# Edges sorted by groups of four nodes instead of by node, with digits spread in bf16 and degrees summed in the first convolution

## The reference

```python
def spline_conv(x, row, col, basis, idx, W, b):       # row = src, col = dst
    z = jnp.einsum('ni,kio->nko', x, W).reshape(N * K, Fout)
    msg = jnp.einsum('es,eso->eo', basis, z[col[:, None] * K + idx])
    out = jax.ops.segment_sum(msg, row, num_segments=N)
    deg = jax.ops.segment_sum(jnp.ones_like(msg[:, 0]), row, num_segments=N)
    return out / jnp.maximum(deg, 1.0)[:, None] + b

h = ones((N, 1))
h = elu(spline_conv(h, ..., stn1_w, stn1_b))          # "c1" and "h1" in the kernel
h = elu(spline_conv(h, ..., stn2_w, stn2_b))          # "c2"
t = elu(h @ stn3_w + stn3_b) @ stn4_w + stn4_b
new_pseudo = clip(pseudo + t[col] - t[row], 0, 1)
x = x + spline_conv(relu(layernorm(x)), ..., new_pseudo's basis, conv_w, conv_b)   # "c3"
x = x + attention over each node's incoming edges, then a gated update            # attention phase
```

## Time and profile before

| | us |
|---|---|
| median of 3 timed runs | 11155.94 |
| lowest and highest | 11149.67, 11158.07 |
| the profiled execution (its span from first to last instruction) | 12528.6 |
| of it, 523 to 3260: `sort_edges` | 2737 |
| of it, 60 to 523: counting | 463 |
| of it, 3450 to 3900: most of c1 | 450 |

### The profile page before, as it was taken

The page is one execution under the profiler, slowest core; times in us unless marked ns, Lnnn a source line. Parts: engine busy times, 40 slices in busy tenths (PEclk is TensorE's granted clock), DMA queues, the critical chain, the costliest instruction groups (busy, mean ns, idle before and its releaser), DMA issues. The chain is left out here.

```text
span 12528.6 us, 178083 instructions
## 1 busy us (share of the span) xinstructions
PE 6505.4 (52%) x38968; PEld 5397.9 (43%) x38968; DVE 7716.2 (62%) x17239; ACT 2933.1 (23%) x8407; POOL 7476.5 (60%) x7456
## 2 busy tenths in 40 slices
PE   3466666666475799999994444545555100000000
PEld 2355555555475677777764434434454100000000
DVE  9844444444498676666664444544576267777777
ACT  0011111111132344344432222322343000000001
POOL 5155555655200888888886888888800566666663
PEclk9966666666698999999997667766777555555555
DMA  1210000000733444444443333333322212221221
GB/s 41 65 36 2 2 2 2 2 2 2 14 41 50 93 93 94 92 94 95 92 93 49 50 51 53 54 50 52 54 42 34 35 49 50 51 50 48 51 54 40
DMA packets 1788557, 605.09 MB, mean 48 GB/s; under 512 B 1595943, under 2 KB 1729575, under 8 KB 1788260
## 3 DMA queue, kind: packets, MB, share of 16 engines
q1 hardware_dynamic: 1078132, 311.05, 12.8%
q0 software_dynamic: 255648, 274.30, 10.7%
q10 hardware_dynamic: 454736, 19.28, 3.0%
HBM read 430.75 MB, written 172.95 MB: 48 GB/s over the span
## 5 line engine op out<-in xcount | busy, mean ns | idle before, releaser
L1222 PE MATMUL c_acc<-c_spread_sb,c_basis_sb 128*125 128x256 f32 (+1 forms) x12544 | 2599.2, 376 | 1502.8 <-issue 655.0
L1222 PEld LDWEIGHTS c_acc<-c_spread_sb,c_basis_sb 128*125 128x125 f32 x12544 | 2266.5, 231 | 1803.5 <-issue 1536.3
L1614 POOL DMA_INDIRECT at_ring<-gat_table,at_place x1568 | 1585.7, 1011 | 1188.5 <-issue 1188.5
L609 POOL DMA_INDIRECT rec<-rk_rec,rk_place x1568 | 1619.3, 1033 | 1110.1 <-DVE rk_place L497 620.7
L1321 ACT ACTIVATE c_sums<-c_acc 125x512 f32<-125x512 f32 (+1 forms) x3136 | 1489.3, 490 | 2258.7 <-PE c_acc L1222 1298.6
L961 POOL DMA_INDIRECT c_ring<-hid_table,c_at x1568 | 1707.1, 1089 | 478.9 <-issue 443.2
L961 POOL DMA_INDIRECT c_ring<-feat_table,c_at x1568 | 1602.7, 1022 | 478.1 <-issue 462.9
L1084 DVE TENSOR_TENSOR c_spread_sb<-c_mark,c_rin 128x512 f32<-128x512 f32 (+1 forms) x3136 | 1745.2, 557 | 60.3
L1871 PE MATMUL gr_hps<-ident,gr_hs 128*32 128x128 f32 x98 | 29.8, 408 | 2473.7 <-issue 2066.3
L492 DVE CUSTOM_DVE_ANT_0 rk_junk_l<-rk_look_ps,rk_hi 128x98 bf16<-128x98 f32 x1568 | 402.2, 257 | 1324.1 <-remote 821.1
L1234 PE MATMUL c_mix<-c_sums,c_w 125*64 125x256 f32 (+1 forms) x9408 | 1037.3, 401 | 187.6 <-issue 133.8
(11 more groups left out here) (356 smaller groups left out, 10126.9 us busy)
## 6 DMA issues: line engine op xcount, KB each, us to landing
c_rin<-rows SPq DMA_DIRECT2D x3136, 42.0 KB
c_rin<-rows SPq DMA_DIRECT2D x3136, 20.0 KB
rows<-c_ring POOLq DMA_DIRECT2D x392, 128.0 KB
rows<-rk_blank SPq DMA_DIRECT2D x112, 252.0 KB
rows<-c_ring POOLq DMA_DIRECT2D x392, 72.0 KB
rows<-at_ring SPq DMA_DIRECT2D x196, 144.0 KB
rec<-rk_rec,rk_place POOLq DMA_INDIRECT x1568
c_ring<-hid_table,c_at POOLq DMA_INDIRECT x1568
```

The lines of the kernel that those rows point to most:

```text
L609: pool.indirect_dma_start(out=d.rec, out_offset=bass.IndirectOffsetOnAxis(ap=place[:, u, j:j + 1], axis=0), in_=rec[:, u, j, :], in_offset ...
L1222: last = pe.matmul(acc[pp % BANKS][:, (w % 2) * WN * feats:(w % 2 + 1) * WN * feats], basis[:, q, w, :, :].rearrange("p a b -> p (a b)"), ...
L1614: pool.indirect_dma_start(out=ring[:, u, j, :], out_offset=None, in_=d.gat_table, in_offset=bass.IndirectOffsetOnAxis(ap=place[:, u, j:j + ...
```

## The change

A *window* is a group of four consecutive nodes; there are 98 x 32 = 3,136 of them (`NWIN`). The change counts and sorts edges by window number (`src >> 2`) instead of by node number:

- The high digit of a window number has 25 values (`NH`) instead of 98. So `cnt_hi` and `rk_hi` are 8 x 25, the running table is [128, 25], and L396, L549, L554, L587 and L492 work on 25 columns. `c.src` in L487 is the window number.
- Rows (L530): instead of one f32 matmul of the node column with the f32 identity, two bf16 matmuls that accumulate: high digit times 128 x identity (`rk_high_ident`), and low digit times identity. ACT copies two digit columns in bf16 instead of one f32 column.
- The degree of each node no longer falls out of the count. c1's weights get a 126th column of ones (`basis_1`), `c1_w` a 126th row and a 65th column, and the 65th output of c1 is the degree; c1's output has rows of 65 values in a tensor of its own (`first_out`).
- In `count_and_prefix` the 98 block starts are taken from the loaded `starts` instead of from `c.base`, so that 12 small DVE instructions move behind the wait for that load.
- Loading has one more pass over `src` on DVE; the weight load of c1 waits for two small DVE writes.

```diff
+NWIN = NB * NW
+WBITS = WN.bit_length() - 1
+NH = -(-NWIN // P)
...
-            chain(dve.tensor_copy(c.src[:, 0:NT], c.src_i[:, :]))
...
+            chain(dve.tensor_scalar(c.key_tmp[:, :], c.src_i[:, :], WBITS, None, ALU.logical_shift_right))
+            chain(dve.tensor_copy(c.src[:, 0:NT], c.key_tmp[:, :]))
...
-        lo_hot, hi_hot = sb("cnt_lo", [P, 2, G, P], BF16), sb("cnt_hi", [P, 2, G, NB], BF16)
+        lo_hot, hi_hot = sb("cnt_lo", [P, 2, G, P], BF16), sb("cnt_hi", [P, 2, G, NH], BF16)
...
-                    dve.tensor_tensor(hi_hot[:, u, :, :], bc(c.ramp_bf[:, 0:NB].unsqueeze(1), [P, G, NB]),
-                                      bc(c.src_hi[:, at].unsqueeze(2), [P, G, NB]), ALU.is_equal).then_inc(made, 1)
+                    dve.tensor_tensor(hi_hot[:, u, :, :], bc(c.ramp_bf[:, 0:NH].unsqueeze(1), [P, G, NH]),
+                                      bc(c.src_hi[:, at].unsqueeze(2), [P, G, NH]), ALU.is_equal).then_inc(made, 1)
...
-            first = turned[0:NB, 0:P].rearrange("p (w n) -> p w n", n=WN)[:, :, 0]
-            chain(dve.tensor_copy(off[:, :], first))
+            chain(dve.tensor_copy(off[:, :], turned[0:NH, 0:P]))
...
+            dve.wait_ge(act_c, 1)
+            chain(dve.tensor_copy(block_fill[:, 0:NB], starts[:, :].rearrange("a (b w) -> a b w", w=NW)[:, :, 0]))
...
-        cols = sb("rk_cols", [P, 2, G])
+        cols = sb("rk_cols", [P, 2, 2, G], BF16)
...
-                        dve.tensor_tensor_reduce(junk_l[:, u, j, :], look[:, j % 2, 0:NB], hi_hot[:, u, j, :], 1.0, 0.0,
+                        dve.tensor_tensor_reduce(junk_l[:, u, j, :], look[:, j % 2, 0:NH], hi_hot[:, u, j, :], 1.0, 0.0,
...
-                    last = pe.matmul(rows[:, u, j, :], bc(cols[:, u, j:j + 1], [P, P]), c.ident[:, :],
-                                     start=True, stop=True)
+                    pe.matmul(rows[:, u, j, :], bc(cols[:, u, 1, j:j + 1], [P, P]), high_ident[:, :],
+                              start=True, stop=False)
+                    last = pe.matmul(rows[:, u, j, :], bc(cols[:, u, 0, j:j + 1], [P, P]), c.ident_bf[:, :],
+                                     start=False, stop=True)
...
-                            pe.matmul(look[:, j % 2, 0:NB], lo_t[:, u, j, :], table[:, k % 2, :],
+                            pe.matmul(look[:, j % 2, 0:NH], lo_t[:, u, j, :], table[:, k % 2, :],
...
-                act.activation(cols[:, u, :], c.src[:, bass.ds(g * G, G)], ACT.Copy).then_inc(cols_made, 1)
+                for k, digit in enumerate((c.src_lo, c.src_hi)):
+                    act.activation(cols[:, u, k, :], digit[:, bass.ds(g * G, G)], ACT.Copy).then_inc(cols_made, 1)
...
-                    last = pe.matmul(acc[u][:, 0:P], basis[:, u, t, :, :].rearrange("p a b -> p (a b)"), mark[:, u, t, :],
+                    last = pe.matmul(acc[u][:, 0:P], basis_1[:, u, t, :], mark[:, u, t, :],
...
-                pe.matmul(back[u][:, 0:HID], sums[:, u, :], wsb[:, :], start=False, stop=True).then_inc(mixed, 1)
+                pe.matmul(back[u][:, 0:HID + 1], sums[:, u, :], wsb[:, :], start=False, stop=True).then_inc(mixed, 1)
```

More of the change, by code:

```diff
@@ new lines, in _ @@
+            for w, slot in enumerate(SLOT_OF):
+                chain(dve.tensor_scalar(need[:, :], block_fill[:, 1:NB + 1], float(P + slot * P - 1), float(EP),
+                                        ALU.add, ALU.min))
+                chain(dve.tensor_copy(c.need[:, w, :], need[:, :]))
+                chain(dve.tensor_scalar(c.need[:, w, :], c.need[:, w, :], (slot * P).bit_length() - 1, None,
+                                        ALU.logical_shift_right))
+            chain(dve.tensor_copy(c.block_start[:, 0, :], block_fill[:, 0:NB]))
@@ L382, in _, with sums @@
             last.then_inc(counted, 1)
-            pe.matmul(count[0][:, 0:NB], c.zeros[:, 0:P], c.zeros[:, 0:NB], start=True, stop=False).then_inc(free, 2)
+            pe.matmul(count[0][:, 0:NH], c.zeros[:, 0:P], c.zeros[:, 0:NH], start=True, stop=False).then_inc(free, 2)
             pe.wait_ge(pe_ready, 1)
-            def sums(k, cnt):
-                pe.matmul(total[:, k * P:k * P + NB], c.ones[:, :], cnt, start=True, stop=True)
-                pe.matmul(within[:, k * P:k * P + NB], c.after[:, :], cnt, start=True, stop=True).then_inc(counted, 1)
-            sums(1, c.base[:, 1, :])
+            def sums(k, cnt, n):
+                pe.matmul(total[:, k * P:k * P + n], c.ones[:, :], cnt, start=True, stop=True)
+                pe.matmul(within[:, k * P:k * P + n], c.after[:, :], cnt, start=True, stop=True).then_inc(counted, 1)
+            sums(1, c.base[:, 1, :], NB)
             with pe.Fori(0, NG // 2) as i:
@@ L548, in _ @@
                         for j in (2 * k, 2 * k + 1):
-                            last = pe.matmul(run[:, 0:NB], lo_hot[:, u, j, :], hi_hot[:, u, j, :],
+                            last = pe.matmul(run[:, 0:NH], lo_hot[:, u, j, :], hi_hot[:, u, j, :],
                                              start=False, stop=True, skip_group_check=True)
@@ L571, in _ @@
             act.wait_ge(updated, 1)
-            act.activation(table[:, 0, :], run[:, 0:NB], ACT.Copy).then_inc(table_ready, 1)
+            act.activation(table[:, 0, :], run[:, 0:NH], ACT.Copy).then_inc(table_ready, 1)
             act.wait_ge(turned, 1)
@@ L586, in _ @@
                         act.wait_ge(updated, g * (G // 2) + k + 2)
-                        act.activation(table[:, (k + 1) % 2, :], run[:, 0:NB], ACT.Copy).then_inc(table_ready, 1)
+                        act.activation(table[:, (k + 1) % 2, :], run[:, 0:NH], ACT.Copy).then_inc(table_ready, 1)
                         if k == 2:
@@ L817, in take @@
                 act.wait_ge(mixed, item + 1)
-                act.activation(conv_out[:, bass.ds(b, 1), :].rearrange("p b o -> p (b o)"), back[u][:, 0:HID], ACT.Copy)\
+                act.activation(conv_out[:, bass.ds(b, 1), :].rearrange("p b o -> p (b o)"), back[u][:, 0:HID + 1], ACT.Copy)\
                     .then_inc(added, 1)
@@ L1903, in dram @@
         return nc.dram_tensor(name, shape, dt).ap()
-    d.off = [dram(f"off{k}", [NB * NW], I32) for k in range(2)]
+    d.off = [dram("off0", [NH * P], I32)]
     d.rec = dram("rec", [EP + TAIL, ROW])
```

140 lines of the change are left out of this document (72 added, 68 removed).

## The result

The changed kernel takes 10986.86 us (median of 4 runs, 10982.12 to 10992.89) against 11156.6 us of the kernel before, a ratio of 0.9842 (95% interval 0.9831 to 0.9854): 170 us less, where 410 were forecast. It is 242 us over the forecast of 10,745, at the upper end of the range (10,560 to 11,000).

What follows compares the result with a forecast made beforehand. The prediction took the sort to be bound by PE and DVE in turn plus a pause, the count by DVE. Count -110 and sort -351 us gave 12,068 us profiled, scaled to 10,745 us timed; range 10,560 to 11,000.

Steps and rivals of the forecast that it cites:

- what bounds the kernel: Sort bound by a loop of waits between PE and DVE, 13.87 us a group, not by POOL; count bound by DVE.
- what is late next: POOL's eight transfers in the sort, some 11.1 to 11.6 us a group, still below the shortened loop of 12.1.
- Count: In the count, DVE's second one-hot array shrinks from 784 to 200 elements: -110 us, bounds -80 to -120.
- Sort: In the sort, four items on the path sum to -1.8 us a group, bounds -0.7 to -2.5: -351 us.
- the bf16 rows: Sort item 3, PE's rows: four bf16 matmuls replace two f32 ones, -0.83 us a group, bounds 0 to -1.1.
- the high array: Sort item 1: DVE's shorter `rk_hi`, which PE's first look-up waits behind, -0.61 us a group.
- item 2: Sort: L492 reads 25 columns instead of 98, -0.38 us a group, bounds -0.1 to -0.6.
- All else: Phases outside count and sort (c1, h1, loading, c2, c3, attention): 0 us, bounds -2 to +8.
- The first one: Rival: POOL or a shorter loop sets the timed sort's pace, only 0 to 0.6 us a group gained: 10,968 us, chance 0.24.
- The pause did not shrink: Rival: the sort's pause shrinks too and the loop falls to POOL's 11 us a group: 10,559 us, chance 0.13.
- it did not double: Rival: the sort's pause comes twice a group, 3.6 us more each: 11,370 us, chance 0.05.
- PE's clock: Rival: less work loses PE's faster clock stretch, the sort gains 1.3 instead of 1.8 us a group: 10,832 us, chance 0.13.

Runs made afterwards that it cites:

- experiment 1: The kernel before, unchanged, profiled a second time: span 11163.1 us, 10.94 us a sort group, POOL waiting 32.3 us for the place.
- wide high array: Changed kernel with only the sort's high one-hot array 98 columns wide again: 0.9844 of the kernel before.
- experiment 6: Changed kernel, sort's low one-hot array in eight instructions, attention's four products a block in twenty or eight: 0.9713 and 0.9742 of the kernel before.
- before's dry pass: Kernel before with an added pass of the sort's loop in which POOL sends one record a group instead of eight: 8.31 us a group.
- after's dry pass: Changed kernel with an added pass of the sort's loop in which POOL sends one record a group instead of eight: 7.46 us a group.
- experiment 4: Both kernels with an added sort pass, POOL sending one record a group instead of eight: 7.46 us a group in the changed kernel, 8.31 in before.
- the kernel with only the sort split: Changed kernel with the sort's low one-hot array made by eight instructions of 128 elements instead of one: 0.9782 of the kernel before.

## Why the prediction was wrong, step by step

**The failing step is the first one: what bounds the kernel.** "POOL sat idle for 620.7 us", so "POOL is not the bound", says the prediction. It took the groups of one profiled execution, in which a sort's group took 13.87 us, as those of the kernel, and put the bound where that execution waited. Run again, before takes 10.94 us a group and POOL waits 32.3 us for the place instead of 620.7 (experiment 1); POOL's own length was the same in both (1,033 and 1,048 ns). The prediction had worked POOL's round out as 11.1 to 11.6 us and called it "what is late next"; it was late already. The sum was then scaled by the ratio of the times, which spreads 1,373 missing us over all phases, where 571 of them were in the sort: 2705.4 us of places against 2133.9.

**Count.** Forecast -110 us, bounds -80 to -120. Measured -117.5 between the traces, +115 when undone. Right: 359 ns for 200 elements against 351, and no price of branches between the arrays (1.42 us a pair is what the two cost back to back).

**Sort.** Forecast -1.8 us a group, scaled to some 312 us. Measured -0.23, 45 us, below the least of its bounds, 0.7. Of its terms: the bf16 rows (0.83, the largest) cost some 20 us instead of giving 162, though a pair's four matmuls take 0.43 us in after (1509.51 to 1509.94), as the prediction has them; the high array (0.61) gave nothing in the sort; item 2 was right in size (a look-up's reduction fell from 257 to 182 ns) and hidden. Sizes read from rows were right, and none was on the path. Without POOL the loop is 0.85 us shorter, at different clocks. Two bounds are added up wrongly: the items' largest give -2.7 us, not -2.5, and the bounds of "all else" stand in the sum with the wrong sign or not at all. It changes the bounds by some 50 us at most and not the forecast.

**All else.** Forecast 0, bounds -2 to +8. Behind the sort's last place the two traces of the changed kernel lie 9.7 us below and 12.0 above the one of before, so no change is shown there.

**Rivals.** The first one had the right bound, with 0.24, and should have had most. Its own evidence was in the text: 1,373 us were missing from the timed runs. What stood against it, that in the count POOL's transfers and PE run side by side and DVE never waits, says nothing of the sort. Its time, 10,968 forecast and 10,987 measured, is in part luck: it took 0.4 us a group for "the shorter arrays beside POOL's first transfer", and 0.23 was measured, of which the shorter high array alone gives nothing (wide high array: 0.9844). The pause did not shrink, it wasn't there; it did not double.

**PE's clock.** This rival's condition came true and cost nothing. The view of the granted clock seems to say the opposite, 0.79 in the second profile of before and 1.00 in after. The stretches from 600 to 2,400 us of before and of after, and of the two kernels of experiment 6, whose sorts are the same to the instruction:

```profile
600.00:2400.00 1800.00, 1127.50 (x7920) 1073.38 (x7920) 1099.57 (x5765) 406.26 (x1648) 1380.75 (x1317) 0.79 0.04 9
```

```profile
600.00:2400.00 1800.00, 1086.51 (x8058) 1046.51 (x8057) 923.65 (x5874) 389.66 (x1845) 1374.22 (x1344) 1.00 0.03 3
```

```profile
600.00:2400.00 1800.00, 1130.17 (x8382) 1088.73 (x8381) 1044.39 (x7325) 406.00 (x1920) 1358.72 (x1395) 0.50 0.03 3
600.00:2400.00 1800.00, 1130.12 (x8383) 1088.52 (x8381) 1044.52 (x7325) 405.69 (x1920) 1358.63 (x1395) 1.00 0.03 3
```

The last two have 0.50 and 1.00 and the same busy time of PE. The eight transposes of a group decide it; they are the same in all kernels. From 600 to 1,800 us (busy us, mean ns) in before's dry pass, granted 0.87; in before, second profile; in after's dry pass, granted 0.50; in the kernel of 0.50 just shown; and in after:

```profile
L508 PE MATMUL dr_lo_ps<-ident_bf,dr_lo 128*128 128x128 bf16 x1152 | 101.9, 240 | 0.0
L522 PE MATMUL rk_lo_ps<-ident_bf,rk_lo 128*128 128x128 bf16 x880 | 103.2, 288 | 0.0
L513 PE MATMUL dr_lo_ps<-ident_bf,dr_lo 128*128 128x128 bf16 x1288 | 165.6, 308 | 0.0
L530 PE MATMUL rk_lo_ps<-ident_bf,rk_lo 128*128 128x128 bf16 x935 | 120.3, 307 | 0.0
L527 PE MATMUL rk_lo_ps<-ident_bf,rk_lo 128*128 128x128 bf16 x896 | 115.2, 307 | 0.0
```

So PE worked at the lower level, 1.2 GHz, all through the sort of after: 307 ns, as where 0.50 is on record. Its trace holds no clock record before 2,552 us, and the view gives 1.00 where there is none. In before PE was at the higher level for part of the time. The lower level goes with the narrow look-ups and table: with the sort made wide again the granted clock is on record, 0.80, and the transposes take 286 ns; with f32 rows alone they take 307. So the clock fell, and the sort got faster all the same, since POOL sets its pace. What part of the missing loop gain of experiment 4 the clock took stays open.

**What would show it.** "If POOL's wait for the place is near nothing, POOL is the bound" is what the trace of after shows (5.3 us), and of the sign that the pause belongs to the profiled execution, the timed runs did their part (170 us saved, 190 named); the profile saved 12528.6 - 10991.2 = 1537 us and not 460, since the pause went with it.

## What to carry to other kernels

If a profiled execution is 12% longer than the timed runs, as here, its waits need not be the kernel's: settle first which waits are its own, by a second profile or, without one, by the engine whose instructions are as long as ever and which would be the bound if the waits were gone. For an engine that issues transfers back to back, multiply the count by the step from one start to the next (here 8 x 1.27 us) and hold it against the loop's time *of the timed runs*; if they are within some per cent, work saved elsewhere is worth little, and what counts is what lengthens a transfer. Look for transfers that are longer than their neighbours and for the instruction beside them; cutting that one in pieces can pay though it costs its own engine time. It paid in the sort of after and in the attention, and not in the sort of before, where a second array follows the first. And hold a granted clock against the length of a matmul of the same shape before you argue from it.

## What the runs showed of the hardware

- One indirect transfer of 128 records of 32 bytes takes POOL 0.97 us and 0.30 us more to the next where nothing holds it; that is 10.2 us for eight, and the best sorts here take 10.32 to 10.33.
- A transfer started beside a DVE instruction with two inputs in SBUF ends 0.84 us after that instruction (0.82 for the attention's gathers), up to 2.02 us long in all beside the single arrays of before. A reduction with one input, 8.91 us long, lengthened none: 552 gathers lie wholly beside one in the trace of the kernel with only the sort split, and they take 0.94 to 0.96 us.
- Short instructions in a row let the first transfer in (1.01 to 1.03 us), but in rows of twelve in bf16 the next one waited for the row's end. In the attention's rows of twenty (256 elements, f32) it did not: of 445 transfers that began beside one, half took 1.16 us or less and 15 over 1.7.
- PE's clock: in the dry pass of after PE was busy 1132.39 of 1,300 us at 0.50; in the dry pass of before 1127.91 of 1,500 us at 0.87. The page "TensorE: Matmul & The Clock Gate" of the Trainium skill (section "Part 1: The HAM clock gate") has activity release the clock. The sorts agree with it, in which less work in look-ups and table went with the lower level. The two dry passes stand the other way round; but the same work keeps PE busy for longer at the lower level, 307 ns a transpose against 240 (both levels mixed), so they don't refute it.
- A granted clock of 1.00 can stand for no record at all: 1.00 and 0.50 were given for the same sort with PE busy 1130.12 and 1130.17 us.
